# Clearing the causal triangle on GpSimd in the first attention of a two-layer decoder, with the mask making in steps between the clearings

## The reference

```python
scores = scale * jnp.einsum('bhqd,bhkd->bhqk', q, k)
mask = jnp.tril(jnp.ones((S, S), dtype=bool))
scores = jnp.where(mask, scores, -jnp.inf)
attn = jax.nn.softmax(scores, axis=-1)
out = jnp.einsum('bhqk,bhkd->bhqd', attn, v)
```

```python
scores = jnp.where(mask == 0, NEG_INF, scores)
```

## Time and profile before

| | |
|---|---|
| median of 3 runs | 3122.18 us (3120.71 to 3127.38) |
| the profiled execution | 3125.54 us |
| its span in the profile | 3123.8 us |
| busy time of PE | 2928.2 us (94%) |
| of DVE | 2260.2 us (72%) |
| of ACT | 1737.3 us (56%) |
| of POOL | 502.8 us (16%) |

### The profile page before, as it was taken

The page is one execution under the profiler, slowest core; times in us unless marked ns, Lnnn a source line. Parts: engine busy times, 40 slices in busy tenths (PEclk is TensorE's granted clock), DMA queues, the critical chain, the costliest instruction groups (busy, mean ns, idle before and its releaser), DMA issues. The chain is left out here.

```text
span 3123.8 us, 94049 instructions
## 1 busy us (share of the span) xinstructions
PE 2928.2 (94%) x39187; PEld 1610.8 (52%) x39187; DVE 2260.2 (72%) x6182; ACT 1737.3 (56%) x2222; POOL 502.8 (16%) x711
## 2 busy tenths in 40 slices
PE   4999999999999999994899999999999999999997
PEld 2566656536545555543455555573333333356664
DVE  6788888587777777748788897227999999743114
ACT  2367767625555565563377777423677777741222
POOL 0156565020000000000222212301100000001114
PEclk8799999979999999997899999998899999999999
DMA  2333333320011001010311111203022221121112
GB/s 73 116 102 108 111 100 105 95 63 24 14 25 25 19 20 26 21 29 17 107 37 42 44 44 36 78 1 96 23 61 53 51 52 48 31 70 63 46 44 88
DMA packets 129385, 172.44 MB, mean 55 GB/s; under 512 B 45215, under 2 KB 99103, under 8 KB 127359
## 3 DMA queue, kind: packets, MB, share of 16 engines
q1 hardware_dynamic: 112688, 119.09, 14.1%
q0 software_dynamic: 10800, 46.76, 4.6%
q10 hardware_dynamic: 5472, 0.56, 0.1%
HBM read 122.76 MB, written 35.16 MB: 51 GB/s over the span
## 5 line engine op out<-in xcount | busy, mean ns | idle before, releaser
L494 PE MATMUL ps<-stack 96*32 96x401 bf16 (+5 forms) x13312 | 1234.6, 355 | 11.5 <-DVE mpart L663 4.0
L514 PE MATMUL ps<-stack 99*32 99x512 bf16 (+3 forms) x11648 | 1116.9, 370 | 55.5 <-DMA stack<-max_parts 24.4
L663 DVE TENSOR_REDUCE mpart<-ps 128x1 f32<-128x512 f32 (+2 forms) x1792 | 1030.5, 618 | 93.6 <-PE ps L494 76.5
L428 ACT ACTIVATE xT<-ps 128x1024 f32<-128x1024 f32 (+3 forms) x800 | 732.1, 938 | 446.6 <-PE ps L514 250.8
L428 ACT ACTIVATE cn<-ps 128x1024 f32<-128x1024 f32 (+4 forms) x800 | 686.1, 870 | 301.6 <-PE ps L514 151.9
L494 PEld LDWEIGHTS ps<-stack 96*32 96x32 bf16 x13312 | 471.5, 96 | 527.2 <-DVE mpart L663 211.6
L659 DVE CUSTOM_DVE_ANT_0 scrap<-ps,arena 128x401 bf16<-128x401 f32 (+1 forms) x1024 | 550.2, 574 | 150.5 <-PE ps L494 126.3
L514 PEld LDWEIGHTS ps<-stack 99*32 99x32 bf16 x11648 | 400.0, 97 | 407.5 <-issue 134.0
L542 PE MATMUL ps<-xT,vall 128*17 128x512 f32 (+4 forms) x3648 | 449.3, 505 | 1.5 <-POOL xT L381 1.0
L542 PE MATMUL ps<-cn,vall 128*17 128x512 f32 (+3 forms) x3392 | 431.2, 496 | 1.9 <-ACT cn L428 0.9
L522 PE MATMUL ps<-arena,big 128*32 128x512 fp8e4 (+1 forms) x3264 | 354.3, 382 | 0.0
(11 more groups left out here) (264 smaller groups left out, 2607.9 us busy)
## 6 DMA issues: line engine op xcount, KB each, us to landing
stack<-q_parts SPq DMA_DIRECT2D x384, 64.0 KB, 2.5
wbuf<-in_mask POOLq DMA_DIRECT2D x16, 800.5 KB, 4.9
stack<-k_parts SPq DMA_DIRECT2D x192, 64.0 KB, 2.7
wbuf<-in_maskT POOLq DMA_DIRECT2D x12, 1024.0 KB, 5.2
arena<-in_moe_w SPq DMA_DIRECT2D x19, 512.0 KB, 4.0
stack<-k_parts SPq DMA_DIRECT2D x192, 50.0 KB, 2.2
stack<-sums_inverse SPq DMA_DIRECT2D x16, 512.0 KB, 6.1
parts<-osb SPq DMA_DIRECT2D x240, 32.0 KB
```

What stands on the lines that cost most here:

```text
L428: nc.scalar.activation(e.prob[tile % P_SLOTS][0:rows, half * HALF + first:(half + 1) * HALF], S_PS(g)[0:rows, first:HALF], ACT.Exp, scale= ...
L494: last = nc.tensor.matmul(bank[quarter(j), 0:w], qs[b][0:KQ, t * P + 32 * j:t * P + 32 * j + 32], ks[b][0:KQ, a:a + w], start=True, stop=True)
L514: last = nc.tensor.matmul(S_PS(g)[quarter(j), lo:hi], ks[b][0:KM, kt * P + 32 * j:kt * P + 32 * j + 32], qs[b][0:KM, half * HALF + lo:half ...
L663: nc.vector.tensor_reduce(dst, src, AX, ALU.max).then_inc(unit_used, 1)
```

## The change

The call for the first causal attention gets `select=True`. The block on GpSimd is rearranged: the making of the masks becomes a function `mask_step(k)`, and one step of it stands behind each clearing. The 16 clearings of a head make 16 steps, and eight steps make one mask tile: step 0 issues its transfer, steps 1 to 3 do nothing, step 4 waits for the transfer, and steps 4 to 7 do a piece each. So a head takes two mask tiles, the first by its key tiles 0 to 7 and the second by 8 to 15. The tiles come in the order t = 0 added, t = 0 turned over, t = 1 added, t = 1 turned over, and so on to t = 12, and then the added tiles 13, 14 and 15, which have no turned-over partner: 29 tiles, in heads 0 to 14.

```diff
+                def mask_step(k):
+                    at, part = divmod(k, 8)
+                    if at >= len(mask_tiles):
+                        return
+                    t, turned = mask_tiles[at]
+                    rows = min(P, S2 - t * P) if turned else P
+                    if part == 0:
+                        if turned:
+                            nc.gpsimd.dma_start(given[0:rows, 0:S], e.d["maskT"][t * P:t * P + rows, :]).then_inc(mask_in, 16)
+                        else:
+                            nc.gpsimd.dma_start(given[:, 0:S2], e.d["mask"][t * P:(t + 1) * P, :]).then_inc(mask_in, 16)
+                    if part < 4:
+                        return
+                    if part == 4:
+                        pool.wait_ge(mask_in, 16 * (at + 1))
+                    if turned:
+                        piece = slice((part - 4) * CH, (part - 3) * CH)
+                        chain.link(nc.gpsimd.tensor_scalar(e.mask_stage[0:rows, piece], given[0:rows, piece], 0.0, None,
+                                                           ALU.is_equal))
+                        chain.link(nc.gpsimd.tensor_copy(e.mask_one[0:rows, t, piece], e.mask_stage[0:rows, piece],
+                                                         saturate=False))
+                    else:
+                        a, n = tiles(S2, -(-S2 // 4))[part - 4]
+                        chain.link(nc.gpsimd.tensor_scalar(e.mask_add[:, t, a:a + n], given[:, a:a + n], 0.0, MASKED,
+                                                           ALU.is_equal, ALU.mult))
...
                 if select:
+                    steps = 0
                     for h in range(H):
                         for n, (kt, rows, half, first, diagonal, last) in enumerate(slots):
                             if diagonal:
...
                                 nc.gpsimd.affine_select(crossed, crossed, [[1, P]], ALU.is_ge, 0.0, base=0,
                                                         channel_multiplier=-1).then_inc(selected, 1)
+                                if masks_ahead:
+                                    mask_step(steps)
+                                    steps += 1
...
         attention_phase(nc, e, S, True, False, [],
                         (None, None, 0), (None, None, 1), (e.w_v, e.xT, False),
-                        [row(e.b_row, "L0_attn_bo")], d["L0_attn_Wo"], e.x_nat, e.eps5, masks_ahead=True,
+                        [row(e.b_row, "L0_attn_bo")], d["L0_attn_Wo"], e.x_nat, e.eps5, masks_ahead=True, select=True,
```

More of the change, by code:

```diff
@@ L352, in _ @@
                         add_bias(t)
+                chain, given = Chain(pool, mask_chain), e.mask_stage.bitcast(I32)
+                mask_tiles = [(t, turned) for t in range(NT) for turned in range(2 if t < NT2 else 1)]
+                def mask_step(k):
[23 more added lines that the diff above has]
+                                                           ALU.is_equal, ALU.mult))
@@ L353, in _ @@
                 if masks_ahead:
                     pool.wait_ge(front_made, len(front))
[L355 to L374, removed]
```

## The result

The changed kernel takes 3223.9 us (median of 4 runs, 3219.4 to 3227.7), the kernel before 3124.8 us on the same chip. The ratio is 1.031, with a 95% interval of 1.030 to 1.033: about 99 us slower. The forecast was 3217 us.

What follows compares the result with a forecast made beforehand. TensorE, busy for 94% of the span, was taken to bound the kernel. Stalls of 96 us plus 23 for the clock minus 25 gained gave +94 on the profiled 3125.54 us, 3219.5, stated as 3217 us; range 3185 to 3252 us.

Steps and rivals of the forecast that it cites:

- The steps stall the products: Key tiles 8 to 15, heads 0 to 13: mask pieces delay clearings and the products behind them, 96 us in all.
- T: Start of the clearing of key tile 12 in a head, the zero point for the times worked out.
- Key tiles 0 to 7 cost nothing: First tile of each head: pieces fit between clearings, which have a further slot before their product; cost 0.
- Heads 8 to 12 go by TensorE's chain, T + 13.1: Next head's first product there follows TensorE's chain from product 15, not the clearing: 6.7 us late.
- The clock, 1.65 us a head: After the last pause of each of 14 heads TensorE runs 3.3 us at half clock: 23 us in all.
- rival 1: First attention: the clock costs nothing, full clock being back at the last pause; +67, 3189 us, chance 0.17.
- list of signs: Expected in the changed profile: some 32 us per head, waits at tiles 13 to 15, clearings 2.5 us apart, lower clock.
- The gain of 25.0 us: First attention: removed matmuls and pauses save the difference to the second attention, 428.3 - 403.3 us.
- The durations of pieces: GpSimd mask pieces take the profiled 1.57 us added and 2.16 us turned over, not the skill page's 0.34 and 0.9.
- rival 4: Between clearings a turned-over piece takes 0.9 us instead of 2.16; 3130 to 3135 us, chance 0.01.
- Rival 2: Mask transfer lands 1 us later in each head and half clock lasts twice as long; 3254 us, chance 0.12.
- Rival 3: Products do not wait, as late clearings fall where TensorE has other work; 3097 us, decided at tile 15, chance 0.03.

Runs made afterwards that it cites:

- swap: Changed kernel with the two mask tiles of heads 0 to 12 in the other order, turned-over one behind key tiles 0 to 7: ratio 1.0256 to the kernel before.
- spread: Changed kernel with both mask tiles' pieces behind key tiles 0 to 7 and the transfers kept away from the maxima: 3106 us, ratio 0.994 to the kernel before.
- the pair of delays: clear_only with two or four GpSimd comparisons behind the clearing of key tile 12 in each head: ratios 1.0007 and 1.0237 to the kernel before.
- clear_only: Changed kernel with the clearings but no mask steps, the mask arrays filled with zeros instead: ratio 0.9947 to the kernel before.
- no_triangle: Kernel before without the matmuls of line 519 and without clearings, masks made as before: ratio 1.0005, attention 394.0 us.
- early_transfer: Changed kernel with the turned-over tile staged in a second place and its transfer issued behind key tile 0: ratio 1.0215 to the kernel before.
- triangle_no_masks: Kernel before with its triangle matmuls but no mask transfers or pieces, mask arrays zero-filled: ratio 1.007, first to last copy 376.2 us.

## Why the prediction was right

The forecast was +94 us and the measurement +99; the attention alone is +98. Against the second causal attention, which the prediction takes as its measure, the changed one is 526.4 - 403.3 = 123 us longer, where the prediction has 96 + 23 = 119. A small slip: 3122.2 + 94 is 3216 us, and the prediction says 3217.

- **The steps stall the products.** Shown. In the head above, against the times worked out: clearing 13 ends at T + 4.8 (4.6), 14 at T + 7.3 (7.1), 15 at T + 9.8 (9.6), the next head's first at T + 13.7 (13.6), and its first product starts at T + 13.8 (13.6). That is 7.4 us late, and with about 1.5 us for the clock, below, it makes up the 9 us by which these heads are longer than the 25.1 us of the second causal attention. In the whole kernel TensorE waits 83.5 us in 48 places for clearings, 80.2 of them in this attention. One expected sign is missing: TensorE has no pause at tile 0 of heads 1 to 8. The product does start 0.1 us behind the clearing's end in each of them, but TensorE, at half clock, is busy with a unit up to that moment. So there the two chains end together, and the biases cost 0.2 us a head instead of 0.5.
- **Key tiles 0 to 7 cost nothing.** Right for the changed kernel: in heads 0 to 12 the waits are at tiles 13, 14, 15 and nowhere else. That there is a limit to it, swap and spread show.
- **Heads 8 to 12 go by TensorE's chain, T + 13.1.** Right in kind, half a microsecond short. In head 9 the clearing of tile 0 is done at T + 12.3 (T = 511.49), and the product comes at T + 13.6: from product 15 it takes 3.65 us at half clock, not 3.5, and product 15 is itself a little late.

```profile
521.42 0.37 PE L555 MATMUL ps<-cn,vall 128*17 128x128 f32 x1 [1.03 <-POOL cn L391]
...
525.07 1.93 PE L555 MATMUL ps<-xT,vall 128*17 128x512 f32 x8
```

- **The clock, 1.65 us a head.** Right: 3.4 us at a clock of 0.56, from the first product of the head shown on, are 1.5 us lost, and the pair of delays gives 1.8 us. So rival 1, by which the clock is back at the last pause, falls. The prediction's own list of signs leaves this term out: it says some 32 us a head, and its sum, 25.1 + 7.2 + 1.65, says 34, which is what was measured.
- **The gain of 25.0 us.** The sum was right, since clear_only ends the attention 23.4 us earlier and the second attention was the right measure. What I expected of its parts, before `no_triangle`, was wrong: 19 us for the matmuls and 6 for meetings of transfers, where the runs show about 3 and 15 between the copies, and the rest in head 0, where TensorE waited 4.5 us for the maxima before and 1.0 us in clear_only. I had read the heads of 26.3 us in the kernel before as free of transfers; all of them have one somewhere.
- **The durations of pieces.** The rows decided, against rival 4: 1.49 and 0.61 us for a turned-over piece, as before, and not 0.9 in all.
- **Rival 2** named a later transfer; it was not later (2.0 us of wait, as worked out), and the half clock lasted no longer behind the last pause. **Rival 3** fails at the place it names: the clearing of tile 15 ends ten microseconds behind T, and the work that TensorE could do meanwhile stands behind product 13 in its fixed order.

Open: how much of the surplus of `early_transfer` (2.5 us a head instead of 1.8) is clock and how much the shorter round of the maxima, as the run changed both.

## What to carry to other kernels

Work given to an engine with spare time is free only where nobody waits for that engine; once a short instruction there gates the critical engine, everything queued in front of it is on the critical path. Look for the gate's densest stretch, not its mean: here the 116 pieces fit behind key tiles 0 to 7 almost without loss, and with about half of them behind 8 to 15 the kernel is 99 us slower. And a large transfer has a place too: keep it away from any small round trip through DRAM that an engine waits for. Where another stage already runs the changed form, measure against that stage, but don't split the difference into parts without a run for each.

## What the runs showed of the hardware that I had not expected

A VectorE instruction stood still while GpSimd filled an array, and over two fills in a row. In `triangle_no_masks` the fills run from 159.9 to 203.6 us, and a VectorE instruction of 16 columns, 0.17 us long as the median of its 64 executions, takes 35.75 us and ends with them; TensorE waits 34 us behind it. Not every instruction is stopped: from 159.9 to 167.8 us, beside the same fill, VectorE's reductions of 512 columns run on at 0.6 to 0.7 us each. The timelines of GpSimd, VectorE and TensorE:

```profile
159.89 21.44 POOL L355 MEMSET arena<- 128x25616 bf16 x1
181.27 22.29 POOL L356 MEMSET arena<- 128x26624 fp8e4 x1
```

```profile
167.84 35.75 DVE L657 TENSOR_SCALAR mneg<-mfin 128x16 bf16<-128x16 f32 x1
```

```profile
203.67 0.62 PE L476 MATMUL ps<-stack 96*32 96x512 bf16 x4 [33.99 <-DVE mpart L635]
```

The Trainium skill, SBUF — State Buffer, section Who interferes with whom, describes a port pair that the two engines share by an exclusive lock, held for one whole instruction. This is what such a lock would look like, except that it lasted over two instructions, and no run here takes it apart further.

A comparison of 401 columns on GpSimd is 1.57 us when it also multiplies and writes bf16, and 1.22 us when it only compares and writes fp32. And a wait of TensorE of 1.5 us once per head left its clock at full, while after one of 4.1 us it was at half.
